# Router logits of a mixture-of-experts block: stationary router, one transpose per group, bias on ScalarE

## The reference

```python
x = x + 0.5 * ffn(layernorm(x))
x = x + attn(layernorm(x))          # linear attention with RoPE and a 5-tap convolution
x = x + 0.5 * ffn(layernorm(x))     # same weights as the first
# ffn(x): a shared gated MLP over all rows, plus 8 routed experts of inner width 256:
logits = x @ router_w.T + routing_bias            # 8 logits a row
scores, indices = top_k(sigmoid(logits), 2)       # two experts a row
scores = scores / sum(scores)
combined = sum over the two: score * down(silu(gate(x)) * up(x))
```

## Time and profile before

| | us |
|---|---|
| median of 3 runs | 471.35 |
| lowest and highest of the 3 | 469.79, 471.42 |
| profiled execution, its own time | 470.26 |
| span of that execution, first to last instruction | 468.5 |

### The profile page before, as it was taken

How to read it: one execution, slowest core, us unless ns; L and a number is a source line. 1 busy time by engine, 2 the same in 40 slices (tenths; PEclk the granted TensorE clock), 3 DMA queues, 4 the chain that set the end, 5 groups by cost and what they waited for, 6 DMA issues and landing times.

```text
span 468.5 us, 9695 instructions
## 1 busy us (share of the span) xinstructions
PE 443.2 (95%) x2959; PEld 377.1 (80%) x2959; DVE 353.5 (75%) x1112; ACT 265.1 (57%) x596; POOL 281.6 (60%) x290
## 2 busy tenths in 40 slices
PE   7999999999999999999899999998899999999992
PEld 3878878888889888879787788887779888887872
DVE  4899996333688978999899999998899743454553
ACT  5965145555766657667533675654285565565630
POOL 4127556777775067713878850777574767763771
PEclk9999999999999999999999999999899999999998
DMA  7991143355422334311113321221443445553332
GB/s 225 366 341 46 55 127 123 99 174 135 127 84 83 92 95 112 109 44 52 57 53 90 96 70 51 69 80 63 124 129 104 135 148 148 152 160 102 95 102 63
DMA packets 74210, 53.62 MB, mean 114 GB/s; under 512 B 9648, under 2 KB 68784, under 8 KB 74160
## 3 DMA queue, kind: packets, MB, share of 16 engines
q1 hardware_dynamic: 65968, 36.19, 26.1%
q0 software_dynamic: 8192, 16.79, 12.1%
HBM read 26.81 MB, written 26.15 MB: 113 GB/s over the span
## 4 chain that ended last, share of the span: by engine, by line
PE 49%; DVE 22%; POOL 12%; issue 8%; DMA 4%; ACT 3%; SPq 0%; POOLq 0%; DVEq 0%; ACTq 0%
PE pool L899 13%; POOL x_sorted L1150 6%; PE gu L847 6%; PE pool L888 6%; PE gu L849 6%; PE gu L848 6%; POOL yg L1170 4%; PE pool L830 3%; DVE X L1236 2%; DVE hs L1213 2%; DVE hs L1217 2%; DVE stats L1247 2%; PE gu L806 1%; ACT xn L1059 1%; DVE xt_lo L1269 1%
## 5 line engine op out<-in xcount | busy, mean ns | idle before, releaser
L1150 POOL DMA_INDIRECT x_sorted<-xn,places x128 | 130.0, 1016 | 64.1 <-issue 33.0
L1170 POOL DMA_INDIRECT yg<-y_sorted,places x128 | 123.7, 966 | 54.2 <-issue 35.7
L1036 ACT ACTIVATE gs<-gu 128x512 f32<-128x512 f32 x124 | 72.4, 584 | 74.3 <-PE gu L849 37.6
L1213 DVE TENSOR_TENSOR hs<-gs,gu 128x512 f32<-128x512 f32 x92 | 60.6, 663 | 59.3 <-ACT gs L1036 58.4
L899 PE MATMUL pool<-w,hT 128*128 x708 | 96.9, 281 | 0.1
L899 PEld LDWEIGHTS pool<-w,hT 128*128 128x128 f32 x708 | 87.4, 191 | 11.3 <-issue 7.7
L847 PE MATMUL gu<-w,xbt_hi 128*128 x177 | 82.4, 465 | 1.5 <-DVE hs L1217 0.9
L849 PE MATMUL gu<-w,xbt_hi 128*128 x177 | 70.3, 397 | 0.0
L848 PE MATMUL gu<-w,xbt_lo 128*128 x177 | 70.2, 396 | 0.0
L1042 ACT ACTIVATE hT<-pool 128x512 f32<-128x512 f32 x92 | 53.3, 581 | 24.0 <-PE pool L888 22.7
L1017 ACT ACTIVATE ys<-pool 128x256 f32<-128x256 f32 x92 | 34.5, 375 | 46.8 <-PE pool L899 46.5
(11 more groups left out here) (137 smaller groups left out, 765.4 us busy)
## 6 DMA issues: line engine op xcount, KB each, us to landing
xb<-x_sorted SPq DMA_DIRECT2D x85, 128.0 KB, 2.4
y_sorted<-ys SPq DMA_DIRECT2D x85, 128.0 KB
x_sorted<-yg SPq DMA_DIRECT2D x6, 512.0 KB, 7.7
X<-x_dram SPq DMA_DIRECT2D x8, 256.0 KB, 4.6
x_sorted<-xn,places POOLq DMA_INDIRECT x128, 2.3
yg<-y_sorted,places POOLq DMA_INDIRECT x128, 2.7
out_dram<-X SPq DMA_DIRECT2D x8, 256.0 KB
raw<-gate_w_dram SPq DMA_DIRECT2D x4, 256.0 KB, 4.9
```

What stands on the lines that cost most here:

```text
L1036: nc.scalar.activation(dst, src, ACT.Silu).then_inc(silu_done, 1)
L1150: nc.gpsimd.indirect_dma_start(x_sorted[g], bass.IndirectOffsetOnAxis(places[g][:, k, t:t + 1], 0), xn[:, b, t % T], None).then_inc(scatte ...
L1170: nc.gpsimd.indirect_dma_start(yg[slot][:, k, t], None, y_sorted[g], bass.IndirectOffsetOnAxis(places[g][:, k, at:at + 1], 0)).then_inc(ga ...
L1213: v.tensor_tensor(hs[n % HB][:].rearrange("p (j i) -> p j i", j=2)[:, 0:k], gs[n % GB][:].rearrange("p (j i) -> p j i", j=2)[:, 0:k], bank ...
```

## The change

The router is now the stationary operand and the transposed rows move. `logits` becomes two matmuls of 512 columns: the router's high and low part (16 columns) by `xt_hi`, then the high part (8 columns) by `xt_lo` added to the first 8 of these rows. The member of number i in its group stands on partitions 32 i to 32 i + 15: the router is held with up to 64 zero columns before it (`MARGIN`), so that the result lands there. `bias` moves to ACT: one activation on 16 partitions by 512 values copies the result into one SBUF tile `logit_rows`, adding the routing bias, which now comes as a value per partition. A new step `logit_turn`, once a group, transposes `logit_rows` back with four TensorE transposes. A new step `halves` on DVE, one reduction for each batch, adds the two halves from PSUM into L. The plan's lengths of many operations are edited and the `URGENCY` string is another one, so all engines' orders differ. Cut to its core:

```diff
+ROWS = 32
+MARGIN = 96
-URGENCY = (
...
+URGENCY = (
...
@@ plan
-        op(("root", l, b), "POOL", 107, ("moments", l, b))
+        op(("root", l, b), "POOL", 120, ("moments", l, b))
-            op(("logits", l, b), "PE", 90, ("lo", l, b), ("cut_router_lo",))
-            op(("bias", l, b), "DVE", 33, ("logits", l, b), ("tables",))
+            op(("logits", l, b), "PE", 47, ("lo", l, b), ("cut_router_lo",))
+            g = group_of(l, b)
+            op(("bias", l, b), "ACT", 58, ("logits", l, b), ("router",), ("logit_turn", g - 1) if g else None)
-            self.op(("front", u, 1), "PE", 73, *needs)
+            self.op(("front", u, 1), "PE", 71, *needs, lands=4)
+        op(("logit_turn", g), "PE", 45, *(("bias", *member) for member in GROUPS[g]))
+        op(("halves", g), "DVE", 17 * len(GROUPS[g]), ("logit_turn", g), ("tables",), ("probs", g - 2) if g >= 2 else None)
+        op(("clamp", g), "DVE", 32, ("halves", g), ("weigh", g - 1) if g else None)
@@ def logits(l, b), PE
-                for t in range(T):
-                    at = slice(t * P, (t + 1) * P)
-                    pe.matmul(dst[:, 2 * t * E:2 * (t + 1) * E], hi[:, at],
-                              router_cut[:].rearrange("p r e -> p (r e)"), start=True, stop=False)
-                    mm = pe.matmul(dst[:, 2 * t * E:(2 * t + 1) * E], lo[:, at], router_cut[:, 0], start=False, stop=True)
-                mm.then_inc(logits_ready[l], 1)
+                once.wait_ge(margin_set, 1)
+                row, i = ROWS * GROUPS[group_of(l, b)].index((l, b)), plan.xt_of[l, b]
+                pe.matmul(pool_ps[m][0:row + 2 * E], router_cut[:, MARGIN - row:], xt_hi[i][:], start=True, stop=False)
+                pe.matmul(pool_ps[m][0:row + E], router_cut[:, MARGIN - row:MARGIN + E], xt_lo[i][:],
+                          start=False, stop=True).then_inc(logits_ready[l], 1)
+            def logit_turn(g):
+                for l, b in GROUPS[g]:
+                    once.wait_ge(logits_read[l], b + 1)
...
+                take(m, halves_done, g + 1)
+                n = ROWS * len(GROUPS[g])
                 for t in range(T):
+                    mm = pe.transpose(pool_ps[m][:, t * P:t * P + n], logit_rows[0:n, t * P:(t + 1) * P], ident[0:n, 0:n])
+                mm.then_inc(logits_turned, 1)
@@ ACT
+            def biased(l, b):
+                g = group_of(l, b)
+                row = ROWS * GROUPS[g].index((l, b))
+                once.wait_ge(logits_ready[l], b + 1)
...
+                wait(once, logits_turned, g)
+                rows = slice(row, row + 2 * E)
+                nc.scalar.activation(logit_rows[rows], misc("logits", l, b)[rows], ACT.Identity,
+                                     bias=bias_rows[rows, 0:1]).then_inc(logits_read[l], 1)
@@ POOL, ahead of its other memsets
+            nc.gpsimd.memset(router_cut[:, 0:MARGIN].bitcast(F32), 0.0).then_inc(margin_set, 1)
+            nc.gpsimd.memset(logit_rows[:], 0.0).then_inc(rows_set, 1)
@@ DVE
-            def biased(l, b):
...
-                v.tensor_tensor(rows, halves[:, :, 0],
-                                rbias_sb.rearrange("p (o e) -> p o e", o=1).to_broadcast([P, T, E]),
-                                ALU.add).then_inc(bias_link[l], 1)
-                once.wait_ge(bias_link[l], b + 1)
-                v.tensor_tensor(rows, rows, halves[:, :, 1], ALU.add).then_inc(logits_read[l], 1)
+            def halves(g):
+                once.wait_ge(logits_turned, g + 1)
...
+                for i in range(len(GROUPS[g])):
+                    ins = v.tensor_reduce(L[g][:, i * T:(i + 1) * T],
+                                          parts[:, :, i, 0:2 * E].rearrange("p t (r e) -> p t e r", r=2), AX.X, ALU.add)
+                ins.then_inc(halves_done, 1)
```

More of the change, by code:

```diff
@@ L62 @@
+    "#mih0tdr}eygD[F1XlF^{M5}^[}y:yu-1}5#}Gd}T#r}.C]wmET}aWaRL`@]}=/]^=3}:M:.}#")
 BLANK = 2 * T * D
@@ L282, in attention @@
         op(("front", nd, 0), "PE", 46, ("front", nd, 1))
[L283 to L287, removed]
+        op(("invert", b), "DVE", 60, ("front", nd, 0), last("scale"))
+        op(("scale", b), "DVE", 68, ("invert", b), last("att_turn"))
+        op(("att_turn", b), "PE", 44, ("scale", b))
+        op(("sum", b), "DVE", 72, ("att_turn", b), ("tap", b, TAPS - 1), last("gate"))
+        op(("gate", b), "DVE", 61, ("sum", b), ("og", b), last("project"))
         op(("project", b), "PE", 90, ("gate", b))
         op(("attended", b), "DVE", 60, ("project", b))
-    HELD = {"turn": "lo", "logits": "bias", "count": "based", "kv": "mask", "v_turn": "vT", "att_turn": "sum", "project": "attended",
+    HELD = {"turn": "lo", "logits": "bias", "logit_turn": "halves", "count": "based", "kv": "mask", "v_turn": "vT", "att_turn": "sum", "project": "attended",
             "pair_turn": "pair_lo", "hidden_turn": "hT_copy", "down": "y_copy", "sdown": "add"}
@@ L332, in stage @@
         return group_of(1, b) + 0.5 if l == 2 else group_of(l, b)
-    ROUTING = ("clamp", "sigmoid", "inverse", "probs", "best", "second", "choose", "count", "based", "place", "table",
+    ROUTING = ("logit_turn", "halves", "clamp", "sigmoid", "inverse", "probs", "best", "second", "choose", "count", "based", "place", "table",
                "weigh")
@@ L998, in _ @@
             multiply_ones(0, WARM)
-            run("PE", {"turn": xn_turn, "logits": logits, "count": count, "regs": find_experts, "pair_turn": pair_turn,
+            run("PE", {"turn": xn_turn, "logits": logits, "logit_turn": logit_turn, "count": count, "regs": find_experts, "pair_turn": pair_turn,
                        "front": front, "hidden_turn": hidden_turn, "down": down, "sdown": shared_down, "kv": kv,
@@ L1106, in cut_router @@
                 once.wait_ge(router_loaded, 16)
-                nc.scalar.activation(router_cut[:, 0], router_raw, ACT.Copy).then_inc(router_hi_done, 1)
+                nc.scalar.activation(router_hi, router_raw, ACT.Copy).then_inc(router_hi_done, 1)
             def cut_shared():
@@ L1292, in clamp @@
                 n = tiles(g)
-                for l, b in GROUPS[g]:
-                    once.wait_ge(logits_read[l], b + 1)
+                once.wait_ge(halves_done, g + 1)
                 v.tensor_scalar(neg[:, 0:n], L[g], -1.0, None, ALU.min)
@@ L1565 @@
     a = {n: np.asarray(v) for n, v in inputs.items()}
+    bias = a["L0_ffn_routing_bias"].reshape(1, E)
+    bias_rows = np.tile(np.concatenate([bias, np.zeros((1, ROWS - E), bias.dtype)], axis=1), P // ROWS)
     arrays = {
```

117 lines of the change are left out of this document (55 added, 62 removed).

## The result

The changed kernel takes 521.1 us (519.4 to 522.3) against 471.3 for the kernel before: the ratio is 1.106, 95% interval 1.102 to 1.110. That is 50 us slower, and 47 us above the top of the predicted range. The forecast was 467.2.

What follows compares the result with a forecast made beforehand. TensorE was taken to bound the kernel, busy 443.2 of 468.5 us. Less 14.4, plus 7.4 and 2.9, saves 4.1: 470.26 becomes 466.2, and 1.09 more for the median gives 467.2; range 460.5 to 474.5.

Steps and rivals of the forecast that it cites:

- The order: All engines' new order: not priceable from the rows; idle time it could win or lose bounded by 25.3 us.
- D: Rival: longer routing chain comes late at an uncovered group, clock falls; likely 474.5, 480 at two places; chance 0.21.
- The TensorE terms: Logits on TensorE: 14.4 us removed, 7.4 added by new matmuls, 2.9 by transposes; net 4.1 less, bounds 2.5 to 6.2.
- DVE and ACT: DVE gets 2.5 us back, not counted in the sum; ACT gains 11.3 us of activations, hidden by its slack.
- POOL's memsets: Two memsets ahead of the first root, up to 1.1 us, covered by POOL's 1.93 us of idleness there.
- The routing chain: From last logits to clamp: 1.6 us longer, a group's scatters 1.6 to 4.7 us later; costed at nothing.
- rival C: TensorE's saving is waited away at the stall before 331, behind POOL's scatters: 471.3, range 469 to 473.5; chance 0.20.
- Rival B: Order gains too: event at 325 to 336 disappears, DVE's relief removes waits; 462.6, range 459 to 465; chance 0.19.
- the clock event at 325 to 336: Two TensorE stalls, 1.57 and 1.34 us, then a lower clock losing 1.7 us; 4.6 us in all.

Runs made afterwards that it cites:

- probs_92: The changed kernel with one plan length put back, the step probs at 92 instead of 104, so only the order changes: 466.4 us, ratio 0.9916.
- new_code_old_order: The changed kernel's code held in the order of the kernel before, only the three new steps placed by the plan: 473.0 us, ratio 1.0056.
- one_character: The changed kernel with one URGENCY character changed, first products of expert pair 25 made late, probs still at 104: 462.0 us, ratio 0.9823.

## Why the prediction was wrong

**The step that failed** is "The order". It said that the rows can't price an order that they don't hold, which was right, and then priced it all the same: "The idle time that an order could win or lose is bounded by what is there: 25.3 us in all". Idleness that is there bounds what an order can win. It bounds nothing that it can lose. The runs show a loss of 55 us (466.4 to 521.1) from 0.12 us in one length of the plan. The forecast "with the same idleness" assumed that a new string with new lengths would be about as good as the old pair; nothing in the rows said so. The plan's own end would have: 509.6 against 461.4, from the two kernels alone. No rival held the loss either: D ended at 480 by one or two late groups. Idleness rose by 43.1 us, and the clock fell behind it.

**The TensorE terms** were near. The sixteen runs of removed matmuls add up to 14.36 us in the kernel before (forecast 14.4). In probs_92 a pair of logits matmuls takes 0.46 to 0.59 us, 0.51 on average without the one behind which TensorE waited, so some 8.2 for sixteen (forecast 7.4, bound 8.8), and the seven turns take 2.46 (forecast 2.9). That nets 3.7 us where 4.1 was forecast. In a fitting order it arrives as 2.9 and 2.8 us, above the lower bound of 2.5; the uncertainty of about 1.6 takes in all of these. The 512-column matmuls stand 0.23 to 0.25 us from start to start at the full clock. The Trainium skill's page "TensorE: Matmul & The Clock Gate", section "Back-to-back issue gap", gives about 131 ns for each such matmul in a stream of weight loads and matmuls. The trace doesn't agree.

**DVE and ACT** were right in size: 2.5 us less forecast for DVE, 3.3 measured as busy time in probs_92 (353.5 to 350.2); ACT 10.8 us for the sixteen activations, forecast 11.3. POOL's memsets hid nearly as forecast: the first root of new_code_old_order starts at 5.28 against 5.19 before, so they are at most 0.1 of the 1.28 us by which its first scatter is late.

**The routing chain**, costed at nothing in the forecast, costs something where the order was not made for it. The first scatter came 1.28 us late, where the chain was forecast to grow by 1.6 to 4.7. With that, new_code_old_order is rival C and the small end of rival D at once: TensorE's gain is waited away, and 2.6 us come on top. What the chain costs alone was not measured; it is somewhere in the difference between a gain of 2.9 us in a fitting order and a loss of 2.6 in the old one, 5.5 us, which also holds what each order favours.

**Rival B** is what probs_92 and one_character show in part: the clock event at 325 to 336 is gone in probs_92 (clock 1.00 in its window from 300 to 360), and the order gained 1.1 us there and 5.5 us in one_character. But the event is not what the order's gain hangs on: one_character, the fastest, still has 0.97 in that window, and new_code_old_order has 1.00 and gained nothing.

## What to carry to other kernels

When a diff changes a searched order and the costs it was searched with, the two are one object: run the planner on the committed pair and compare its end with that of the kernel before, before any chip time. The list scheduler here is so sensitive that a step longer by 0.12 us moved the result by some 35 us in one kernel and 55 in the other, so a string should be written down as the order itself, which no later edit of a length can break. And judge an edit of the work with the order held in both directions: here the same edit cost 2.6 us in the old order and won 2.8 and 2.9 us in orders made for it, all of it invisible behind 50 us.

## What the runs showed of the hardware

The stationary operand's load gets shorter with its columns. In the changed kernel (count, busy us, mean ns), and below it two of the three loads of 80 columns (start, us):

```profile
L941 PEld LDWEIGHTS pool<-xt_hi,router_cut 128*16 128x16 f32 x7 | 0.7, 94 | 2.1 <-DVE xt_lo L1292 2.0
...
L941 PEld LDWEIGHTS pool<-xt_hi,router_cut 128*80 128x80 f32 x3 | 0.5, 182 | 0.1
```

```profile
37.80 0.15 PEld L941 LDWEIGHTS pool<-xt_hi,router_cut 128*80 128x80 f32 x1
...
267.97 0.25 PEld L941 LDWEIGHTS pool<-xt_hi,router_cut 128*80 128x80 f32 x1
```

The mean of 182 ns mixes two clocks: at the full one a load of 80 columns takes 0.15 us, and the third stands in a stretch at the lower clock. The router's load of 16 columns takes 94 ns, and the old one of 128 columns (line 941 before) took 193. I had given this no worth, and no run shows one.

An activation of 512 values costs 677 ns on 16 partitions with one bias from a tile. That is 83 ns over the plain copy's 594 on 128 partitions and 137 under the 814 of the one with two such operands; so 16 partitions in place of 128 bring no saving that these rows show, and partitions and operand were not measured apart.

A lower clock adds busy time: from 266.69 to 267.12, behind the longest stall, two 512-column matmuls stand 0.43 us apart in place of 0.23. The changed kernel's TensorE was busy for 13.7 us more than probs_92's with the same 2,891 instructions, at a mean granted clock of 0.940 against 0.997.
